# A transformer block with top-2 experts on one core: expert outputs added to the output by an accumulating scatter, in place of a mixing stage

## What is computed

```
q  = ln(x);  x = x + self_attention(q, q)              # 16 heads of 16, 1024 keys
qc = ln(x);  x = x + cross_attention(qc, ln(context))  # 77 keys
h  = ln(x)
vals, idx = top_k(h @ router_w.T + router_b, 2)        # 8 experts
gates = softmax(vals)
eo[e] = gelu(h @ fc1[e].T + b1[e]) @ fc2[e].T + b2[e]  # 256 -> 1024 -> 256
out = x + gates[0] * eo[idx[0]] + gates[1] * eo[idx[1]]
```

## Time and profile before

| what | us |
|---|---|
| median of 3 runs | 1809.44 |
| lowest and highest | 1798.57, 1811.01 |
| the profiled execution | 1805.67 |
| its span, first to last instruction | 1803.8 |
| PE busy in the span | 1460.4 (81%) |
| DVE busy | 1187.7 (66%) |
| ACT busy | 842.6 (47%) |
| POOL busy | 544.2 (30%) |

### The profile page before, as it was taken

The page is one execution under the profiler, slowest core; times in us unless marked ns, Lnnn a source line. Parts: engine busy times, 40 slices in busy tenths (PEclk is TensorE's granted clock), DMA queues, the critical chain, the costliest instruction groups (busy, mean ns, idle before and its releaser), DMA issues. The chain is left out here.

```text
span 1803.8 us, 28831 instructions
## 1 busy us (share of the span) xinstructions
PE 1460.4 (81%) x9972; PEld 758.0 (42%) x9973; DVE 1187.7 (66%) x1711; ACT 842.6 (47%) x1708; POOL 544.2 (30%) x387
## 2 busy tenths in 40 slices
PE   5884699999999999998467888753499999999950
PEld 3442122222222222221333444432388888888850
DVE  4553799999999999992364666414665555555526
ACT  2221388888888888887123335420022222222210
POOL 1001999999810000000222221000133333333310
PEclk8996699999999999999677778655599999999985
DMA  3546746574412122000554555335611212111229
GB/s 111 175 152 176 175 121 168 141 210 135 141 36 79 45 44 78 2 1 30 131 121 114 146 158 153 105 128 198 234 48 58 59 59 59 59 59 59 59 86 317
DMA packets 141094, 199.52 MB, mean 111 GB/s; under 512 B 24792, under 2 KB 102873, under 8 KB 139467
## 3 DMA queue, kind: packets, MB, share of 16 engines
q1 hardware_dynamic: 119563, 140.13, 27.5%
q0 software_dynamic: 17216, 54.02, 9.4%
q10 hardware_dynamic: 4224, 4.19, 0.7%
HBM read 118.76 MB, written 78.80 MB: 110 GB/s over the span
## 5 line engine op out<-in xcount | busy, mean ns | idle before, releaser
L1091 DVE TENSOR_REDUCE sa_half_maxs<-sa_psm 128x2 f32<-128x1024 f32 x512 | 604.8, 1220 | 60.5 <-PE sa_psm L959 51.5
L1075 ACT ACTIVATE sa_p<-sa_pss 128x512 f32<-128x512 f32 x1024 | 532.7, 604 | 100.8 <-PE sa_pss L1002 100.7
L1002 PE MATMUL sa_pss<-sa_q,sa_k 49*128 49x512 f16 x1024 | 312.7, 385 | 18.1 <-DMA sa_q<-sa_max_row 10.3
L1017 PE MATMUL sa_pso<-sa_p,sa_v 128*32 128x512 f32 x2048 | 274.5, 608 | 18.8 <-ACT sa_o L1053 9.4
L959 PE MATMUL sa_psm<-sa_k,sa_q 48*128 48x512 f16 x1024 | 261.7, 396 | 30.0 <-DMA sa_k<-dram_sa_qk_parts 18.9
L2266 ACT ACTIVATE moe_h<-moe_psh,moe_b 128x256 f32<-128x256 f32 x312 | 122.1, 474 | 319.3 <-PE moe_psh L2203 243.5
L1002 PEld LDWEIGHTS sa_pss<-sa_q,sa_k 49*128 49x128 f16 x1024 | 77.7, 94 | 333.4 <-ACT sa_p L1075 267.0
L2201 PE MATMUL moe_psh<-moe_hh,w_high 128*128 128x256 f16 x624 | 170.7, 274 | 0.0
L2203 PE MATMUL moe_psh<-moe_hh,w_low 128*128 128x256 f16 x624 | 170.7, 274 | 0.0
L2202 PE MATMUL moe_psh<-moe_hl,w_high 128*128 128x256 f16 x624 | 170.7, 274 | 0.0
L2217 PE MATMUL moe_pse<-w_high,moe_h1h 128*128 x624 | 170.1, 273 | 0.3 <-DVE moe_h1l L2292 0.3
(11 more groups left out here) (202 smaller groups left out, 1926.8 us busy)
## 6 DMA issues: line engine op xcount, KB each, us to landing
sa_w_stage<-in_w POOLq DMA_DIRECT2D x32, 512.0 KB, 5.2
dram_sa_v<-qkv_v_sb SPq DMA_DIRECT2D x8, 1024.0 KB, 5.3
dram_sa_qk_parts<-qkv_part SPq DMA_DIRECT2D x16, 512.0 KB, 6.6
sa_v<-dram_sa_v SPq DMA_DIRECT2D x16, 512.0 KB, 5.8
dram_w_high<-sa_w_high POOLq DMA_DIRECT2D x32, 256.0 KB, 2.5
dram_w_low<-sa_w_low POOLq DMA_DIRECT2D x32, 256.0 KB, 3.3
dram_sa_raw<-sa_o SPq DMA_DIRECT2D x4, 2048.0 KB, 9.5
dram_ca_raw<-x_o_sb SPq DMA_DIRECT2D x8, 1024.0 KB, 5.1
```

The lines of the kernel that those rows point to most:

```text
L1002: pe.matmul(ps_s[place % SBANKS][:], k_st[u][rows, j0 + j, kt * kp:(kt + 1) * kp], q_st[u][rows, j0 + j, half * HALF:(half + 1) * HALF], s ...
L1017: mm = pe.matmul(ps_o[h * VW:(h + 1) * VW, :], v_st[u][:, kt, v_at:v_at + VW], probs[n % PSLOTS][h][:], start=(kt == 0), stop=(kt == key_t ...
L1075: act.activation(probs[n % PSLOTS][h][:], ps_s[place % SBANKS][:], ACT.Exp, scale=float(DH) ** -0.5).then_inc(read, 1)
L1091: dv.tensor_reduce(half_maxs[U % 2][:, at % 2, :, c], ps_m[z][:], AX_X, ALU.max).then_inc(taken, 1)
```

## The change

1. The mixing stage is gone, and with it the scratch tensors of x2 and of the expert outputs. Cross-attention stores x2 straight into out. Routing writes the gates to a table in memory, `gate_rows`, with one 4-byte row for each (choice, token). In the expert stage POOL gathers a tile's 256 gates (two more indirect DMAs per tile), DVE multiplies `eo` by them (one more wait and two more operations per tile), and the scatter adds into out with `compute_op=ALU.add`. Both choices of a token hit the same row of out, so each scatter first waits until the scatter of the tile before has landed. Padding slots have a target past the end and are skipped.
2. In the projections DVE's `normalise` moves from the head of step t to before `finish` of step t - 1.
3. In self-attention SP issues load(2) and load(3) after place_row(0) and place_row(1), one in each of the first two units.

```diff
@@ tokens_program, vector
         def step(t, has):
-            if has(0):
-                normalise(*t)
...
             if qk and has(-1):
                 low_parts(*at(t, -1), range(QC // 2, QC))
             if weights and has(0):
                 cut_low(*t)
+            if has(1):
+                normalise(*at(t, 1))
             if has(-1):
                 finish(*at(t, -1))
@@ attention_phase, sync
-                for L in range(1, slots):
-                    load(L)
+                load(1)
                 place_row(0)
                 for U in range(units):
                     G, half = divmod(U, 2)
+                    if U < slots - 2:
+                        load(U + 2)
                     if U + 1 < units:
                         place_row(U + 1)
@@ route_phase, sync, scalar, tensor, vector
+                                 (place_no, "place_no"), (spare, "spare"), (ident, "ident")):
...
+                sp.wait_ge(gates_kept, 1)
+                sp.dma_start(gate_rows.rearrange("(t p) a -> t (p a)", p=P), gates_turned[:]).then_inc(gates_stored, 16)
                 sp.wait_ge(w_loaded, 16 * 4 * E)
+                sp.wait_ge(gates_stored, 16)
...
+                act.wait_ge(gates_ready, 2)
+                act.activation(gates_turned[:], ps_gates[:], ACT.Copy).then_inc(gates_kept, 1)
...
+                pe.wait_ge(gates_ready, 1)
+                pe.transpose(ps_gates[:], gates[:].rearrange("p k t -> p (k t)"), ident[:]).then_inc(gates_ready, 1)
...
-                dv.wait_ge(consts, 16 * 9)
+                dv.wait_ge(consts, 16 * 10)
...
-                step(dv.tensor_copy(numbers_i[:], row_to[:]))
-                step(dv.tensor_tensor(target_f[:], row_to[:], spare_to[:], ALU.add))
-                own()
-                step(dv.tensor_scalar(tokens[:], numbers_i[:], N - 1, None, ALU.bitwise_and))
-                step(dv.tensor_copy(targets[:], target_f[:]))
-                own()
+                step(dv.tensor_copy(rows[:], row_to[:]))
+                step(dv.tensor_copy(spare_i[:], spare_to[:]))
+                own()
+                step(dv.tensor_scalar(tokens[:], rows[:], N - 1, None, ALU.bitwise_and))
+                own()
+                step(dv.tensor_tensor(targets[:], tokens[:], spare_i[:], ALU.bitwise_or))
+                own()
@@ expert_phase, gpsimd
+                def gather_gates(t):
+                    u = t % 2
+                    if t >= 2:
+                        pool.wait_ge(eo_ready[u], t // 2)
+                    for j in range(JT):
+                        pool.indirect_dma_start(
+                            out=gate[u][:, j:j + 1], out_offset=None, in_=gate_rows,
+                            in_offset=bass.IndirectOffsetOnAxis(
+                                ap=rows[:, t * JT + j:t * JT + j + 1], axis=0)
+                        ).then_inc(gate_loaded[u], 16)
                 def scatter(t):
                     u = t % 2
                     pool.wait_ge(eo_ready[u], t // 2 + 1)
+                    if t >= 1:
+                        pool.wait_ge(stored[1 - u], 16 * JT * ((t + 1) // 2))
                     for j in range(JT):
                         pool.indirect_dma_start(
-                            out=eo_dram, out_offset=bass.IndirectOffsetOnAxis(
+                            out=out_dram, out_offset=bass.IndirectOffsetOnAxis(
                                 ap=targets[:, t * JT + j:t * JT + j + 1], axis=0),
-                            in_=eo[u][:, j, :], in_offset=None).then_inc(stored[u], 16)
+                            in_=eo[u][:, j, :], in_offset=None, bounds_check=N - 1, oob_is_err=False,
+                            compute_op=ALU.add).then_inc(stored[u], 16)
                         gather(t)
                     if t >= AHEAD:
                         scatter(t - AHEAD)
+                    if AHEAD - 2 <= t < T + AHEAD - 2:
+                        gather_gates(t - AHEAD + 2)
@@ expert_phase, vector
                     dv.scalar_tensor_tensor(eo[u][:], ps_e[u][:], 1.0 / W_SCALE,
                                             b2[u][:, None, :].broadcast_to([P, JT, D]),
-                                            ALU.mult, ALU.add).then_inc(eo_ready[u], 1)
+                                            ALU.mult, ALU.add).then_inc(biased[u], 1)
+                    dv.wait_ge(gate_loaded[u], i * 16 * JT + 16 * JT)
+                    dv.wait_ge(biased[u], i + 1)
+                    for j in range(JT):
+                        mm = dv.tensor_scalar(eo[u][:, j, :], eo[u][:, j, :], gate[u][:, j:j + 1], None, ALU.mult)
+                    mm.then_inc(eo_ready[u], 1)
@@ combine_phase is removed; build
-        combine_phase(nc, x2, eo, gates, out)
```

More of the change, by code:

```diff
@@ L1955, in _ @@
                 own()
-                step(dv.tensor_tensor(gates[:, 1, :], gates[:, 0, :], gap_exp[:], ALU.mult))
+                dv.tensor_tensor(gates[:, 1, :], gates[:, 0, :], gap_exp[:], ALU.mult).then_inc(gates_ready, 1)
                 dv.wait_ge(counted, 1)
@@ L2412, in build @@
                        for part in ("high", "low")] for w in (1, 2))
-            route_phase(nc, logits, gates, tokens, targets, tile_expert, a, w_cut, (w1, w2))
-            expert_phase(nc, xhat, tokens, targets, eo, tile_expert, (w1, w2), a["b1"], a["b2"],
+            route_phase(nc, logits, gate_rows, rows, tokens, targets, tile_expert, a, w_cut, (w1, w2))
+            expert_phase(nc, xhat, rows, tokens, targets, gate_rows, out, tile_expert, (w1, w2), a["b1"], a["b2"],
                          a["moe_ln_g"], a["moe_ln_b"], ident)
-        combine_phase(nc, x2, eo, gates, out)
 def laid_out(inputs):
```

69 lines of the change are left out of this document (15 added, 54 removed).

## The result

The changed kernel takes 1851.11 us (median of 4 runs, 1850.44 to 1852.94), the kernel before 1806.62 us beside it (1798.57 to 1811.01). The ratio is 1.0253, 95% interval 1.0213 to 1.0293: slower, where 1747 us was forecast. The profiled execution has a span of 1848.6 us, against 1803.8.

What follows compares the result with a forecast made beforehand. PE was taken to bound the expert stage, with mixing behind it at a DMA share of 0.93. 1805.67 - 19 - 10.3 - 56.1 + 1.3 + 24.5 = 1746, set at 1747 us for the median; range 1716 to 1790.

Steps and rivals of the forecast that it cites:

- Projections, -19: Projections: normalise 2.3 us earlier shrinks PE's gap in six of eight blocks, 14.1 us, plus a clock share: -19 us.
- The clock part: Projections: the shorter gap may keep PE's clock up in Q and K groups; 5 us taken, between 0 and 6.5.
- Start of self-attention, -10.3: Self-attention's start: row 0's DMAs no longer queue behind load(2) and load(3), so PE's wait goes: -10.3 us, or -6.
- The end, -56.1: Kernel end: without mixing, the end comes at 1747.7 after gating, two scatter issues and a plain scatter's landing: -56.1 us.
- the 3.5 us kept for the bound: Kernel end: the adding scatter's landing might exceed the plain one's by 0 to 3.5 us; 0 taken.
- Routing, +1.3: Routing: one more constant, a dependent step and the gates' store behind the weight loads: +1.3 us (0.5 to 2.5).
- The expert stage, +24.5: Expert stage: 3.36 us added to POOL's chain uses its 3.5 us slack; 0.68 us a tile over 36 tiles: +24.5 us.
- The bound of 59 us: Expert stage: upper bound of the loss, (2.2 + 0.6 + 0.5) / 2 x 36 = 59 us.
- rival 3: Expert stage: adding-scatter issues from 2.65 us lose the whole gain; at 3.2 us the time is 1828; chance 0.08.
- Rival 2: Expert stage: new DMAs cost twice the issue in the scatter, +1.0 us a tile, or gelu comes later: 1783; chance 0.18.
- Rival 1: Expert stage: POOL's chain does not bind, output comes on time and the stage keeps 452 us: 1722; chance 0.24.
- Rival 4: Projections and self-attention: order changes do nothing because the next late thing refills the gap: 1776; chance 0.05.

Runs made afterwards that it cites:

- e4: Changed kernel with a scatter that does not add, into a scratch (expert sum and residual left out of the output): 1833.0 us, single run.
- e9: Changed kernel with AHEAD = 4 for 3 and a scatter that does not add, into a scratch: 1803.8 us, single run.
- e12: e9 plus a 640-column memset on GpSimd and a wait for it ahead of each of a tile's two scatters: 1729.3 us, single run.
- e13: e9 plus a 64-column memset and a wait for it ahead of each of GpSimd's six DMAs of a tile: 1720.9 us, single run.
- e1: Kernel before with only the two order changes (normalise in the projections, loads at the start of self-attention): 1771.4 us, ratio 0.9844 to the kernel before.
- e2: Changed kernel with AHEAD = 4 for 3, so the gather of tile n + 4 is issued ahead of the scatter of n: 1723.8 us.
- e3: Changed kernel, AHEAD = 3, with the two gate gathers put behind the gather of x in GpSimd's queue: 1728.4 us, single run.
- e11: Changed kernel with every gate gather issued twice, the second into a tile nobody reads: 1935.4 us, single run.
- e14: e6 plus a 64-column memset and a wait for it ahead of each of the two scatters: 1881.4 us, single run.
- e6: Kernel before plus two unused four-byte gathers per tile, placed where the change has its gate gathers: 1892.1 us, single run.

## Why the prediction was wrong

- **Projections, -19:** right in mechanism. -20.85, with the short gap and the clock as described, and just past the end of the part's range (-14 to -20.5). The clock part, taken at 5, is at its full size.
- **Start of self-attention, -10.3:** right to the tenth.
- **The end, -56.1:** -51.6. Two adding scatters and the later start cost 1.6 us more than taken, and from the last issue to the end of the span are 6.4 us, not 3.5: of the 3.5 us kept for the bound, 2.9 were needed. With the plain scatter at the same place (e4, e9, e12, e13) these are 4.3 us, so 2.1 of the 2.9 are the adding scatter's longer landing, which I had taken at nothing.
- **Routing, +1.3:** the stretch from the first instruction of routing to the next stage's first issue grew from 49.4 to 49.9 us. Cross-attention was 3.3 us shorter in the profile after, which I had not forecast. Since e1's median gains only 29 us and profiles differ by 5 us ahead of the experts, it may be no effect at all.
- **The expert stage, +24.5:** this is the step that failed, by its size. From the first turn to the last output the stage took 131.4 us more (578.4 against 447.0). The place and the mechanism were those forecast: the chain through POOL's queue with 3.5 us of slack for two turns; e2 and e3 show it. What was mis-sized is the overrun of a pair. Most of it came from terms that the prediction put at the plain row's price (the adding issue, the landing) or had in no term at all (the low clock behind the wait, the later start of a bounded scatter). For a pair I had 22.56 - 0.14 + 0.9 + 0.6 = 23.9 us, and 29.9 were measured. The 6.0 us between them, from the rows of both traces:

| term of a pair | taken | measured | short by |
|---|---|---|---|
| two adding scatters, issue | 1.94 | 3.21 | 1.3 |
| start of a bounded scatter behind its wait | 0.3 | 0.8 | 0.5 |
| POOL's issues stretched beside DVE | 0.6 | 2.0 | 1.4 |
| landing of the x gather | 2.05 | 3.40 | 1.35 |
| from turn to output, at the low clock after the wait | 11.21 | 13.59 | 2.4 |
| output late, because Gelu is late | 0.9 | 0 | -0.9 |

  18 pairs of 6.0 us make 108 us, and with the 24.5 taken 132. That this comes so near to 131.4 is in part luck: the mean pair is 0.3 us shorter than this one, and 3.5 us of the loss lie in the stage's first turns (12.9 us apart for 9.4), which are no pair of the chain. The bound of 59 us was too tight because it was the sum of the terms of its own list, each at its worst, with the adding issue at the plain price even there, and left out what a wait itself brings.
- **The sum:** 1747 + 107 (experts) + 4.5 (end) - 0.8 (routing) - 1.9 (projections) - 3.3 (cross) is 1852.5; measured 1851.1.
- **The rivals:** rival 3 (an adding issue at 2.65 us or more) came out on the right side with the wrong price: the issue costs 1.6 us, and the point at which the whole gain is gone was passed by five small terms together. Rival 2 had the price of the new DMAs nearly right (0.64 us over the plain one, not 1.0) but stopped there. Rival 1 is refuted by the waits: turns waited 108.3 us for gathers of x, against 12.4 before. Rival 4 is refuted by e1.

The Trainium skill ("SBUF — State Buffer", section "Who interferes with whom") had been weighed with the cast alone, since it says that a tensor_tensor with both inputs in SBUF takes only the read side that it shares with GpSimd, and infers that descriptor generation needs the write side. The rows of the pair differ: an issue beside the cast (1530.38) took 1.91 us, and the next one, beside the TENSOR_TENSOR of 1531.64, took 1.99, against 1.01 and 1.03 beside neither. The second of them began after the cast had ended. The measurement decides, and the stretch to reckon with is that of both instructions. Whether it is the reading of the row numbers (an indirect DMA has them in an SBUF tile) or the writing of descriptors that is held up, no run here shows.

## What to carry to other kernels

Find what stands in a queue between an instruction that waits for late work and an instruction that feeds early work, and keep the second ahead of the first; here one number (AHEAD = 4) was worth 127 us, and a cheaper scatter in the old order only 18, net of TensorE's pauses (e4). When slack is used up, don't price only what was added: the wait brings the low clock, and each further consequence adds to the same chain, so a forecast at the edge of the slack needs a range up to the full sum of them. Before you blame a late engine, see whether anyone waits for it: in e9 ScalarE was late in 29 of 39 tiles, and the time was lost in a layer of TensorE that waits for nobody. And a busy share says nothing of this: POOL was busy 54% of the slow stage and 76% of the fast one.

## What the runs showed of the hardware

- An indirect scatter that adds takes 1.60 us to issue in the mean of the changed kernel and of e2 (1.73 in e11), the plain one 1.02 in e4 and e9. With a bounds check it starts 0.5 us later behind a wait (0.81 for 0.28, e13 and e14). From the end of its last issue to the end of the span are 6.44 us, and 4.33 with the plain one. Off the critical path (e2) none of this held TensorE.
- Four-byte indirect gathers of 128 rows are no cheaper to issue than gathers of 1 KB rows (0.97 to 1.0 us undisturbed), so 78 of them are 100 us of GpSimd's time.
- When GpSimd issues six plain indirect DMAs back to back (7.4 us in e6), ScalarE starts up to 5 us after the matmuls that it waits for, and TensorE pauses for 0.5 to 1 us at a time inside layer 2. The pauses are what costs: 72 us of the 79 us of expert length between e9 and e2, with ScalarE's lateness hidden. With adding scatters (1.6 us) and AHEAD = 4, or with the pauses of e12 and e13, layer 2 is back at 200 to 201 us. The Trainium skill ("SBUF — State Buffer", section "Who interferes with whom") says that PE and ACT never wait on anyone at SBUF's ports, so the ports would not explain it. No run here shows which resource does. It stays open, as does why the short pauses ahead of all six DMAs were enough (e13) but not those ahead of two (e14).
